# Extra context rows from 32-bit weights, first chunk compared ahead of the scores, and a reordered preparation in a cross-attention and feed-forward kernel

## The reference

```python
kv_dca = (y_dca @ Wkv_dca + bkv_dca).reshape(b, DCA, 2, H, HD)
k_dca = _ln(kv_dca[:, :, 0], kn_dca_w, kn_dca_b)
v_dca = kv_dca[:, :, 1]
q = _ln((x @ Wq + bq).reshape(b, s1, H, HD), qn_w, qn_b)
...
ctx = _attn(q, k, v) + _attn(q, k_dca, v_dca)
x = x + ctx @ Wo + bo
h = silu(ln(x) @ lut[gate_idx].T) * (ln(x) @ lut[up_idx].T)
x = x + h @ lut[down_idx].T
```

## Time and profile before

| | |
|---|---|
| median of 3 runs | 813.15 us |
| the profiled execution | 814.19 us |
| its span, first to last instruction | 811.9 us |
| mean granted TensorE clock, share of 2.4 GHz | 0.989 |
| TensorE busy | 758.9 us, 93% |
| VectorE busy | 511.8 us, 63% |
| ScalarE busy | 492.5 us, 61% |
| GpSimd busy | 254.2 us, 31% |

### The profile page before, as it was taken

The page is one execution under the profiler, slowest core; times in us unless marked ns, Lnnn a source line. Parts: engine busy times, 40 slices in busy tenths (PEclk is TensorE's granted clock), DMA queues, the critical chain, the costliest instruction groups (busy, mean ns, idle before and its releaser), DMA issues.

```text
span 811.9 us, 14838 instructions
## 1 busy us (share of the span) xinstructions
PE 758.9 (93%) x5842; PEld 310.5 (38%) x5842; DVE 511.8 (63%) x991; ACT 492.5 (61%) x1001; POOL 254.2 (31%) x267
## 2 busy tenths in 40 slices
PE   2887786899999999999999999999999999999998
PEld 1342231333444333234443342335433433365445
DVE  7979989899877994224769963228499810153211
ACT  3479987788646886663558876645488856511100
POOL 6883221000853332003852320025623300014320
PEclk9999999899999999999999999999999999999999
DMA  7749969487430000321300003222000000100001
GB/s 253 194 131 270 266 168 279 116 182 169 132 74 1 1 2 27 78 54 59 94 34 1 1 14 67 52 78 53 3 1 1 2 27 27 40 14 1 0 14 40
DMA packets 74244, 61.22 MB, mean 75 GB/s; under 512 B 33408, under 2 KB 60800, under 8 KB 73920
## 3 DMA queue, kind: packets, MB, share of 16 engines
q1 hardware_dynamic: 73840, 60.02, 27.9%
q10 hardware_dynamic: 208, 0.26, 0.1%
q0 software_dynamic: 128, 0.00, 0.0%
HBM read 43.29 MB, written 10.55 MB: 66 GB/s over the span
## 4 chain that ended last, share of the span: by engine, by line
PE 78%; DVE 12%; ACT 4%; issue 3%; POOL 2%; DMA 1%; SPq 0%; DVEq 0%; POOLq 0%; ACTq 0%
PE ps L1677 52%; PE ps L2028 8%; PE ps L2009 6%; PE ps L1980 5%; PE ps L1728 4%; DVE arena L1122 3%; ACT ps L1005 2%; DVE nmax L1472 2%; PE ps L2015 2%; PE ps L1876 2%; POOL hrstd L684 1%; DMA arena<-idx 1%; DVE stat L1159 1%; DVE nmax L1477 1%; DVE arena L1129 1%
## 5 line engine op out<-in xcount | busy, mean ns | idle before, releaser
L1677 PE MATMUL ps<-arena,wf_hi 128*128 128x512 f16 (+2 forms) x736 | 211.0, 371 | 0.8 <-issue 0.8
L1005 ACT ACTIVATE ps<-ps,nmax 128x496 f32<-128x496 f32 x256 | 166.3, 652 | 23.2 <-DVE nmax L1477 23.2
L1037 ACT ACTIVATE arena<-ps 128x1024 f32<-128x1024 f32 x128 | 124.3, 1026 | 73.1 <-PE ps L2015 73.1
L1677 PE MATMUL ps<-arena,wf_lo 128*128 128x512 f16 (+2 forms) x368 | 136.1, 370 | 0.0
L1677 PE MATMUL ps<-wf_hi,arena 128*128 128x512 f16 (+3 forms) x374 | 114.8, 368 | 0.5 <-DVE arena L1129 0.3
L684 POOL TENSOR_TENSOR hrstd<-hvar,mhalf 128x16 f32<-128x16 f32 (+1 forms) x33 | 101.1, 3078 | 41.1 <-DVE hvar L1226 40.9
L1677 PEld LDWEIGHTS ps<-arena,wf_hi 128*128 128x128 f16 (+1 forms) x736 | 69.6, 100 | 85.7 <-issue 21.6
L1122 DVE TENSOR_SCALAR arena<-arena,wf_lo 128x2048 f16<-128x2048 f16 (+1 forms) x132 | 89.6, 739 | 8.3 <-PE ps L1728 4.6
L633 POOL TENSOR_TENSOR xrstd<-xvar,mhalf 128x1 f32<-128x1 f32 x32 | 23.8, 744 | 202.0 <-DVE xvar L1164 202.0
L1728 PE MATMUL ps<-arena,wf_lo 128*32 128x512 f16 (+1 forms) x1056 | 66.6, 394 | 12.6 <-ACT arena L832 7.1
L1677 PE MATMUL ps<-wf_lo,arena 128*128 128x512 f16 (+3 forms) x187 | 68.5, 366 | 0.0
(11 more groups left out here) (153 smaller groups left out, 1039.9 us busy)
## 6 DMA issues: line engine op xcount, KB each, us to landing
arena<-idx SPq DMA_DIRECT2D x124, 128.0 KB, 3.8
arena<-in_x SPq DMA_DIRECT2D x32, 256.0 KB, 2.8
wf_lo<-in_idx SPq DMA_DIRECT2D x10, 512.0 KB, 5.4
idx<-wf_hi SPq DMA_DIRECT2D x10, 384.0 KB, 3.7
out<-arena SPq DMA_DIRECT2D x15, 256.0 KB, 2.0
wf_lo<-in_idx SPq DMA_DIRECT2D x11, 256.0 KB, 6.9
arena<-in_ctxT SPq DMA_DIRECT2D x5, 512.0 KB, 3.8
v_next<-arena SPq DMA_DIRECT2D x8, 256.0 KB, 5.7
```

Source lines behind the costliest of these rows:

```text
L1005: last = act.activation(sc, sc, ACT.Exp, bias=nmax[:, 0, t, h:h + 1], accum_out=den[:, 0, t, h:h + 1])
L1037: act.activation(probs[n_ % 2][:, 2 * p:2 * p + 2, :], ps[:, bank:bank + 2, :], ACT.Exp).then_inc(s["probs_set"], 1)
L1677: last = pe.matmul(dst, l, r, start=(first and i == 0), stop=(stop and i == len(todo) - 1))
```

## The change

The extra rows are no longer split into 16-bit halves. Their context slice is scaled by 256 in place, in 32 bits, and multiplied with the 32-bit weights as loaded; the weights are not centred, and instead the 64 projected key rows are centred in the accumulator (`extra_centre(a)`). The comparisons of the first chunk are taken out of the first pair of the scores and put into VectorE's preparation list. The lists of all engines for the first batch's preparation are reordered: GpSimd's first two conversions stand ahead of and behind its first head power, `value_bias` stands behind `query_low(1)`, TensorE's first two value products stand between the first projections. The load of Wo moves behind the last projection and the last value product. GpSimd's later conversions get other chunk counts. In the third batch VectorE's list has two entries moved. The core of the diff:

```diff
-cd = [sb(f"cd{i}", [P, KC, MD], F16) for i in range(2)]
...
 sum_b, sum_k = cut(H), cut(KC * H)
-sum_d = cut(KC * H).rearrange("p (k h) -> p k h", k=KC)
...
     load_rep(1)
-    sp.wait_ge(s["wd_lo"], 1)
-    sp.dma_start(st_o.rearrange("p (k n) -> p k n", k=G), by_chunk("Wo")).then_inc(s["wo_in"], 16)
...
     sp.wait_ge(s["proj_done"], nth_unit((0, 0), len(UNITS_0)))
+    sp.wait_ge(s["v_done"], nth_value((0, 0), len(values_of((0, 0)))))
+    sp.dma_start(st_o.rearrange("p (k n) -> p k n", k=G), by_chunk("Wo")).then_inc(s["wo_in"], 16)
     sp.dma_start(ctx_early.rearrange("p (k n) -> p k n", k=KC),
                  A["ctxT"][1].rearrange("(k p) n -> p k n", p=P)).then_inc(s["ctx_in"], 16)
...
         if prev is None:
+            norm(1, 0, (0, 0))
+            selectors()
+            lookup_constants()
+            shift_patterns()
+            norm(1, 1, (0, 0))
+            norm(1, 2, (0, 0))
+            convert(0)
             rstd(0)
-            convert(0)
-            for u in range(1, len(units)):
-                rstd(u)
             convert(1)
+            rstd(1)
+            rstd(2)
+            norm(1, 3, (0, 0))
+            rstd(3)
+            rstd(4)
+            rstd(5)
+            rstd(6)
+            rstd(7)
+            rstd(8)
             low_half(a, 7, 0)
             convert(2, 1)
             context_low(2)
             convert(3, 3)
-            low_half(a, 8, 4)
-            convert(4, 5)
+            convert(4, 4)
+            convert(5, 5)
             dca_shift(a, 0, 6)
-            convert(5, 7)
+            low_half(a, 8, 6)
+            convert(6, 7)
             second_context_low(0, 8)
             second_context_low(1, 9)
             dca_shift(a, 1, 10)
-            convert(6, 11)
-            convert(7, 12)
-            convert(8, 13)
+            convert(7, 11)
+            convert(8, 12)
+            convert(9, 13)
             dca_shift(a, 2, 14)
-            convert(9, 15)
-            convert(10, 16)
+            convert(10, 15)
         elif sum(a) == 1:
...
     nothing = lambda slot: None
-    norm(1, 0, (0, 0))
-    selectors()
-    norm(1, 1, (0, 0))
-    lookup_constants()
-    shift_patterns()
-    norm(1, 2, (0, 0))
-    norm(1, 3, (0, 0))
-
     core((0, 0), nothing, nothing, (0, 1), None)
...
             act.wait_ge(s["k_evac"], T)
+        elif units_of(a)[u][0] == "d":
+            act.wait_ge(s["kd_cent"], 1)
         else:
             act.wait_ge(s["proj_done"], nth_unit(a, u + 1))
...
                 between(u)
         else:
+            turn(1, 0, LB0[0])
             query_hi(0)
-            turn(1, 0, LB0[0])
             query_hi(1)
             act.wait_ge(s["b_cent"], 1)
             act.wait_ge(s["bias_in"], 16 * 7)
             act.activation(b16[:, :], st_b, ACT.Copy, scale=WS).then_inc(s["b_hi"], 1)
             query_hi(2)
-            query_hi(3)
-            turn(1, 1, LB0[1])
             act.wait_ge(s["wv_in"], 16)
             act.activation(fl(wv[0]), st_kv[1], ACT.Copy, scale=WS).then_inc(s["wv_hi"], 1)
-            act.wait_ge(s["cd_in"], 16 * KC)
-            act.activation(cd[0].rearrange("p k n -> p (k n)"), ctx_dca, ACT.Copy).then_inc(s["cd_hi"], 1)
+            turn(1, 1, LB0[1])
             context_hi(a, ctx_first, cT)
+            query_hi(3)
             act.wait_ge(s["sq_eps"], 1)
             square(a, 0, True)
             act.wait_ge(s["wk_cent"], 1)
             act.activation(fl(wk[0]), st_kv[0], ACT.Copy, scale=WS).then_inc(s["wk_hi"], 1)
+            values(0)
+            act.wait_ge(s["cd_in"], 16 * KC)
+            act.activation(ctx_dca, ctx_dca, ACT.Copy, scale=WS).then_inc(s["cd_hi"], 1)
             square(a, 1, True)
             square(a, 2, True)
-            square(a, 3, True)
-            values(0)
-            act.wait_ge(s["wd_cent"], 1)
-            act.activation(wd[0][:, :, :], st_d, ACT.Copy, scale=WS).then_inc(s["wd_hi"], 1)
-            values(1)
-            turn(1, 2, LB0[2])
             act.wait_ge(s["par_set"], 1)
             rescale(0)
+            turn(1, 2, LB0[2])
+            square(a, 3, True)
             square(a, 4, True)
             rescale(1)
+            values(1)
+            rescale(2)
             square(a, 5, True)
-            rescale(2)
-            values(2)
+            turn(1, 3, LB0[3])
+            square(a, 6, True)
             rescale(3)
-            square(a, 6, True)
-            turn(1, 3, LB0[3])
             rescale(4)
             square(a, 7, True)
+            values(2)
+            values(3)
             rescale(5)
-            values(3)
             square(a, 8, True)
...
             low_half(0)
-            low_half(1)
             residual(2, prev)
             moments(2, 2, prev, rows_of(2))
             normalise(a, 2, False)
+            low_half(1)
+            normalise(a, 3, False)
             standardise(2, 2, prev, rows_of(2), ln2[2])
             residual(3, prev)
             moments(2, 3, prev, rows_of(3))
             stage(2, 2, prev)
-            normalise(a, 3, False)
             variance(a, 4)
...
             moments(1, 0, a, x_first[0])
             query_sums(0)
+            standardise(1, 0, a, x_first[0], x_first[0])
             query_centre(0)
             query_sums(1)
-            standardise(1, 0, a, x_first[0], x_first[0])
             moments(1, 1, a, x_first[1])
             query_centre(1)
             query_sums(2)
+            query_centre(2)
             query_low(0)
-            moments(1, 2, a, x_first[2])
-            query_centre(2)
+            bias_sums()
+            bias_centre()
             query_sums(3)
-            bias_sums()
+            turn(1, 0, a, LB0[0])
             standardise(1, 1, a, x_first[1], x_first[1])
-            bias_centre()
+            query_low(1)
+            value_bias()
+            query_low(2)
             query_centre(3)
-            query_low(1)
-            turn(1, 0, a, LB0[0])
-            query_low(2)
             bias_low()
             query_low(3)
+            values_low()
+            moments(1, 2, a, x_first[2])
             key_sums()
-            moments(1, 3, a, x_first[3])
-            key_centre()
             turn(1, 1, a, LB0[1])
             variance(a, 0)
+            key_centre()
             context_lo(a, ctx_first, cT)
-            value_bias()
             key_low()
-            standardise(1, 2, a, x_first[2], x_first[2])
-            extra_context_low()
             variance(a, 1)
             normalise(a, 0, True)
-            values_low()
+            standardise(1, 2, a, x_first[2], x_first[2])
+            parameters()
             variance(a, 2)
-            extra_sums()
-            extra_centre()
-            parameters()
             normalise(a, 1, True)
+            moments(1, 3, a, x_first[3])
+            turn(1, 2, a, LB0[2])
             variance(a, 3)
-            extra_low()
             normalise(a, 2, True)
+            variance(a, 4)
             low_half(0)
-            turn(1, 2, a, LB0[2])
-            variance(a, 4)
             low_half(1)
             standardise(1, 3, a, x_first[3], x_first[3])
+            extra_centre(a)
             normalise(a, 3, True)
             variance(a, 5)
             normalise(a, 4, True)
             low_half(2)
-            low_half(3)
             variance(a, 6)
             turn(1, 3, a, LB0[3])
+            one_hot(0, (0,))
             normalise(a, 5, True)
+            low_half(3)
+            one_hot(0, (1,))
+            variance(a, 7)
             low_half(4)
-            variance(a, 7)
             normalise(a, 6, True)
             low_half(5)
+            one_hot(0, (2,))
             variance(a, 8)
             dve.wait_ge(s["tr_lo"], UNITS_0.index(("d", 0)) + 1)
             for i in range(2):
                 dve.tensor_copy(kT[i][:, :, 0:DCA], kd[i][:, :, 0:DCA]).then_inc(s["kd_set"], 1)
             normalise(a, 7, True)
             low_half(6)
+            one_hot(0, (3,))
 
 
...
+    def extra_centre(a):
+        u = units_of(a).index(("d", 0))
+        kd_ps = heads(ps[0:MD, proj_bank(a, u), :])
+        dve.wait_ge(s["proj_done"], nth_unit(a, u + 1))
+        dve.tensor_reduce(sum_d, kd_ps, AX_X, ALU.add).then_inc(s["kd_sum"], 1)
+        dve.wait_ge(s["kd_sum"], 1)
+        dve.scalar_tensor_tensor(out=kd_ps, in0=spread(sum_d), scalar=-1.0 / HD, in1=kd_ps, op0=ALU.mult, op1=ALU.add)\
+            .then_inc(s["kd_cent"], 1)
...
         for c in lookups_in(slot):
-            if c < NCH - 1:
+            if 0 < c < NCH - 1:
                 one_hot(c, (0,) if c == NQ - 1 else range(NJ))
 
...
             if kind == "d":
-                pe.wait_ge(s["cd_lo"], 1)
-                pe.wait_ge(s["wd_lo"], 1)
+                pe.wait_ge(s["cd_hi"], 1)
+                pe.wait_ge(s["wd_in"], 16)
                 n_ = MD
-                keys = [(both(lambda a_: cd[a_][:, i, :]), both(lambda a_: wd[a_][:, i, 0:D])) for i in range(KC)]
```

(49 more changed lines are left out.)

## The result

The changed kernel takes 818.69 us (median of six runs, 817.89 to 819.95), the one before 812.88 in the same runs; the ratio is 1.0066 with a 95% interval from 1.0052 to 1.0080. It is slower by 5.8 us. The profiled execution took 819.12, its span is 816.9: 5.0 longer than before's.

| mark | before, us | after, us | later by |
|---|---|---|---|
| first maxima of the scores | 55.70 | 65.01 | 9.3 |
| turns behind the last scores (PE, `caug`) | 144.72 | 151.61 | 6.9 |
| the 2851st matmul from the end (third batch) | 370.25 | 377.02 | 6.8 |
| the 2701st matmul from the end | 402.95 | 407.87 | 4.9 |
| last matmul | 808.95 | 813.91 | 5.0 |

The account below looks back on a forecast made before the run. Up to 145 us it took VectorE, then TensorE products, then VectorE to set the pace; afterwards TensorE. Scores' start +8.3, clock +2.5, stall −3.9 made +6.9 on 814.19: 821.1, as median 820.0; range 814 to 824.

Parts of the forecast that it names:

- The wait that comes: In the preparation, VectorE's bias sum, moved forward, would wait for the second bias array from 15.8 to 22.5: 6.7 us.
- The walk from 22.5 us: Preparation after the wait: first value product at 32.7, scores starting at 63.1 instead of 54.8, 8.3 us later.
- rival (b): In the preparation, biases land in time; scores start about 1.7 us late, stall gone, −2.2 in all: 811; chance 0.12.
- The clock: TensorE idle from 27.3 to 32.7; a lower-clock stretch where the long chain of products begins: 2.5 us lost.
- The 32-bit products: Extra rows' keys and values on TensorE: together 0.9 us more (0.8 to 1.4).
- the gain from less VectorE work: Preparation: VectorE has about 3.7 us less arithmetic before the scores, not where time is set: 0 (bound 0.8).
- The first chunk: First score pairs: the four comparisons (2.9 us) stood in a gap that stays, so moving them gains 0.1.
- The stall that goes: Scores, chunk at 122.87 us: VectorE's 3.49 us transfer wait goes, and 0.37 us waiting for TensorE: gain 3.9.
- low_half of unit 8 two chunks later is wanted only at pair twelve: nothing: Scores: GpSimd's later low half of unit 8 was claimed to cost nothing.
- Nothing in the diff touches a queue's order after that: Beyond the first 145 us: TensorE almost always busy from 150 us, the rest shifts unaltered.

Follow-up runs that it names:

- b_bias: The kernel before with only value_bias moved forward, right behind query_low(1) in VectorE's list; 818.02 us, ratio 1.0064.
- a_order: The changed kernel with the second query projection ahead of the first value product in TensorE's list; 815.39 us, ratio 1.0032 to the kernel before.
- a_bias: The changed kernel with value_bias put back behind context_lo in VectorE's list; 814.36 us, ratio 1.0014 to the kernel before.
- a_clock: The changed kernel with 48 additional small matmuls on TensorE between the first query projection and the first value product; 817.33 us.
- a_chunk: The changed kernel with the first chunk's four comparisons back in the first pair of the scores; 818.69 us.
- a_convert: The changed kernel with GpSimd's later conversions and unit 8's low half at the old chunk counts and places; 819.48 us.
- a_third: The changed kernel with the third batch's VectorE list in its old order; 820.54 us.
- b_wide: The kernel before with the 32-bit products of the extra rows alone, Wo loaded behind the last products; 813.49 us, ratio 0.9998.
- b_convert: The kernel before with GpSimd's later conversions at the new chunk counts, unit 8's low half left where it was; 808.81 us, ratio 0.9945.
- a_unit8: The changed kernel with unit 8's low half back behind GpSimd's conversion of block 3, chunk count 4; 816.46 us.
- a_best: The changed kernel with value_bias, unit 8's low half put back and the second query projection ahead of the first value product; 807.56 us.
- b_best: The kernel before with the conversions' new chunk counts and the third batch's new VectorE order, unit 8's low half left in place; 807.54 us.

## Why the prediction was right, point by point

The direction and the place were right: 820.0 against 818.69, a loss of 6.9 us against 5.8 (5.0 in the profiled span). Some terms were off, and two were missed that nearly cancel. That the sum came so close is luck in part: against the marks the start of the scores was put 1.5 us too late (10.8 for 9.3), the stall's gain 1.3 too small, and 2.9 of loss and 1.9 of gain were left out, together 1.8.

- **The wait that comes.** VectorE stood from about 16.4 to 21.8 instead of 15.8 to 22.5; the array landed 3.95 us after the issue, not 4.9 as in the row of before. Shown by b_bias: 4.59 us of wait, 4.75 at the scores. The figure of about 2 us per transfer in the Trainium skill (page "DMA: Bandwidth & Descriptors", section "Anatomy of one DMA — SWDGE (gpsimd) path") is for transfers that GpSimd issues; this array, issued by SyncE behind others, took 3.95 to 4.9 us in the traces, while the kernel's 256 KB stores of the output land in 2.0.
- **The walk from 22.5 us.** Value product 0 was expected at 32.7 and came at 32.25; scores, clock included, at 65.6, and came at 64.08. The walk took the queue order right, and a_order showed its part, 3.8 us. In rival (b) I gave the order, with the 32-bit products, only 1.7; a_bias measures 4.3. That rival's price was mis-sized: had the biases come in time, the change would still have been no gain.
- **The clock.** 2.5 expected, 2.1 to 2.6 measured (a_clock). The size was right, the way to it only in part: the prediction has the clock fall in the gap that begins at 27.3 us. In the changed kernel's trace it had not risen before, and in those of a_chunk, a_convert and a_third it fell at 22.2 to 23.3, ahead of that gap, in or right behind one of 2.8 to 4.3 us in the first projection, and stayed low for 13.7 us. The gap did not lower the clock; with TensorE busy in it the clock was up by 29.4 (a_clock). The Trainium skill's rule that the lower rate is the default which activity lifts (page "TensorE: Matmul & The Clock Gate", section "What's actually happening") agrees with that run: 48 useless matmuls in the gap gave time back.
- **The 32-bit products.** 0.9 us was the price on TensorE; 1.93 us per product is within the bounds, but at the scores it came to 0.0 (b_wide), where the products started 1.1 us earlier. That the gain from less VectorE work, which I took as 0, cancelled this price is likely; no run separates the two. The prediction also calls GpSimd "nearly as full" as TensorE from 24.2 to 54.8 us, but the row has it fuller, 29.47 us busy against 28.53, and in b_wide VectorE waits for it.
- **The first chunk.** 0.1 expected, nothing measured (a_chunk), and the chain that I named is what leaves the gap.
- **The stall that goes.** 3.9 expected, 5.2 measured in the kernel before (b_convert), 3.4 in the changed one (a_convert). The mechanism held, but for the 0.37 us put down to the lower clock, which b_wide has not in spite of the stall; the sum left out that the last conversion no longer runs beside VectorE's small arithmetic (1.0).
- **The step that failed: "low_half of unit 8 two chunks later is wanted only at pair twelve: nothing".** It asked only who needs the unit's data. ScalarE's early write of a value tile waits on the same count for its buffer's sake, five pairs earlier. 2.2 to 2.9 us (a_unit8).
- **The other that failed: "Nothing in the diff touches a queue's order after that".** The third batch's two moved entries do. And TensorE was not busy for all but a few tenths in each 100 us: from 300 to 400 us it was busy for 98.36, so idle for 1.6, and 1.37 of these are the wait that the change took away. 1.9 to 2.5 us gained (a_third).

The account by the experiments: +9.3 (wait 4.8 to 5.0, order 3.8, 0.5 over) +2.9 (unit 8) −5.2 (conversions) −1.9 (third batch) = +5.1, against 5.0 between the spans. The half microsecond over is within the 1.0 us by which the start of the scores differs between executions; with both repairs made (a_best) 0.2 is left of the 9.3. That the account closes to 0.1 is luck too: by the ratios of the runs the same five parts are 5.2, 2.8, 2.1, −4.5 and −2.0, together 3.6 against 5.4, each known to 1 or 2 us. What stays open is how much less the conversions are worth once the scores start later (3.4 against 5.2), of which the lower clock behind the turns explains 0.8 us.

## What to carry to other kernels

An instruction that takes 0.2 us and whose result is wanted much later still holds its whole queue while it waits: before moving it forward, compare its new place with the landing time of what it reads. When a step is moved back, look up every wait on the counter that it raises, not only who reads its data; buffers are guarded by the same counts. And where a change is a bundle, price its parts one by one: here two parts were worth 5.2 and 1.9 us, three cost 4.8, 3.8 and 2.9 (each by one trace), and the 32-bit products and the first chunk, which gave it its name, nothing.

## What was unexpected of the hardware

TensorE's share of granted clock reads 1.00 ahead of the first change that the profile records (at 37.57 us in the changed kernel), though six 512-column matmuls at 32.25 us take 2.72 us and the same six 1.46 later; there the clock has to be read from durations:

```profile
32.25:37.57 5.32, 5.32 (x13) 1.92 (x14) 1.05 (x1) 0.79 (x2) 2.89 (x2) 1.00 1.13 271
```

And a conversion on GpSimd and an instruction on VectorE hold each other up. Beside the last conversion a VectorE instruction of 64 columns took 1.34 us instead of 0.29. The comparisons of 2,048 columns take 0.74 us each as a rule, but longer where they start while a conversion runs: in the changed kernel the first of the four at 92.66 us took 1.24, and ended 0.55 behind the conversion that began at 91.89; in a_bias and b_best such comparisons took 1.81, 1.64 and 1.60, each ending 0.55 behind the conversion.

```profile
92.66 3.23 DVE L1126 TENSOR_SCALAR arena<-arena,wf_lo 128x2048 f16<-128x2048 f16 x4
```

In a_clock the comparison began first (92.58): it kept its 0.74 us, and the conversion behind it (92.79) took 1.86 instead of 1.46.
